# An order of TensorE's work made by a model of the engines, in place of fixed quarters of each key tile

## The reference, cut to what matters

```python
x = x + L0_xattn(layernorm(x), ctx)     # softmax(q k / sqrt(8)) v, then an output projection
x = x + L0_ffn(layernorm(x))            # 8 gated experts, hidden 192, capacity 512
x = x + L1_xattn(layernorm(x), ctx)     # softmax
x = x + L1_ffn(layernorm(x))            # 8 gated experts, hidden 256, two loops with rmsnorm
x = x + L2_xattn(layernorm(x), ctx)     # sigmoid(scores) v, no softmax
x = x + L2_ffn(layernorm(x))            # 8 experts with gelu, hidden 512
x = x + L3_xattn(layernorm(x), ctx)     # softmax
x = x + L3_ffn(layernorm(x))            # 8 gated experts with biases, hidden 256
```

## Time and profile before

| | |
|---|---|
| median of the runs shown | 4472.9 us (4469.91 to 4476.91, n = 3) |
| span of the profiled execution | 4471.6 us |
| ACT, PE, DVE, POOL busy | 87%, 86%, 65%, 18% of the span |
| mean granted TensorE clock | 0.968 of full |

### The profile page before, as it was taken

How to read it: one execution, slowest core, us unless ns; L and a number is a source line. 1 busy time by engine, 2 the same in 40 slices (tenths; PEclk the granted TensorE clock), 3 DMA queues, 4 the chain that set the end, 5 groups by cost and what they waited for, 6 DMA issues and landing times.

```text
span 4471.6 us, 69696 instructions
## 1 busy us (share of the span) xinstructions
PE 3844.3 (86%) x26742; PEld 881.7 (20%) x26742; DVE 2892.4 (65%) x5746; ACT 3897.2 (87%) x4328; POOL 820.2 (18%) x705
## 2 busy tenths in 40 slices
PE   8888888988889888898979998888888888888886
PEld 2121112211122211222212221111111111112112
DVE  6878898788877788877603332110785588877823
ACT  4689998899988899889899899989987889888994
POOL 3110001510035200252512111111001110044002
PEclk7699999999999999999999999999999999999998
DMA  6220001100021110111102221110011000010001
GB/s 157 56 63 25 12 12 33 35 12 12 17 60 31 46 25 17 33 36 34 33 19 63 64 71 27 39 40 17 14 31 27 27 12 12 14 43 24 5 1 50
DMA packets 124482, 151.31 MB, mean 34 GB/s; under 512 B 29272, under 2 KB 76384, under 8 KB 124080
## 3 DMA queue, kind: packets, MB, share of 16 engines
q1 hardware_dynamic: 123424, 146.41, 12.2%
q10 hardware_dynamic: 720, 0.40, 0.0%
HBM read 123.21 MB, written 23.51 MB: 33 GB/s over the span
## 4 chain that ended last, share of the span: by engine, by line
PE 49%; ACT 27%; DVE 13%; issue 6%; DMA 1%; SPq 0%; POOL 0%; ACTq 0%; POOLq 0%; DVEq 0%
PE av L884 20%; ACT prob L1045 17%; DVE mpart L1156 10%; PE scores L874 8%; PE side L906 5%; ACT above L1053 5%; PE scores L984 4%; PE side L1002 4%; PE side L984 2%; DVE above L1160 2%; PE scores L897 1%; ACT ag L1096 1%; ACT tx L1087 1%; PE side L874 1%; PE scores L1026 1%
## 5 line engine op out<-in xcount | busy, mean ns | idle before, releaser
L1045 ACT ACTIVATE prob<-scores 128x1024 f32<-128x1024 f32 x2998 | 2948.2, 1036 | 249.1 <-PE scores L874 221.8
L1156 DVE TENSOR_REDUCE mpart<-side 128x1 f32<-128x512 f32 (+1 forms) x3456 | 2132.8, 657 | 625.6 <-PE side L906 613.1
L884 PE MATMUL av<-prob,VA 128*9 128x512 f32 x6528 | 867.5, 604 | 40.5 <-ACT prob L1045 37.5
L884 PE MATMUL av<-prob,VB 128*9 128x512 f32 x6528 | 864.8, 602 | 18.7 <-ACT prob L1045 17.9
L874 PE MATMUL scores<-QP,KA 32*128 32x512 f16 x2996 | 562.0, 390 | 145.8 <-ACT above L1053 81.7
L874 PE MATMUL scores<-QP,KB 32*128 32x512 f16 x3000 | 554.3, 385 | 144.3 <-ACT above L1053 71.1
L906 PE MATMUL side<-KA,QP 32*128 32x512 f16 (+1 forms) x2112 | 618.1, 390 | 41.9 <-DVE mpart L1156 34.2
L906 PE MATMUL side<-KB,QP 32*128 32x512 f16 (+1 forms) x2112 | 578.1, 379 | 35.8 <-DVE mpart L1156 32.9
L1160 DVE CUSTOM_DVE_ANT_0 above<-side,above 128x512 f32<-128x512 f32 x768 | 516.3, 686 | 79.3 <-PE side L906 65.2
L1053 ACT ACTIVATE above<-scores 128x1024 f32<-128x1024 f32 x384 | 394.1, 1026 | 113.1 <-DVE mpart L1160 59.0
L1045 ACT ACTIVATE prob<-side 128x1024 f32<-128x1024 f32 x266 | 288.5, 1085 | 24.3 <-PE scores L874 23.8
(11 more groups left out here) (197 smaller groups left out, 2713.0 us busy)
## 6 DMA issues: line engine op xcount, KB each, us to landing
cwb<-weights SPq DMA_DIRECT2D x80, 256.0 KB, 3.9
KA<-kstacks SPq DMA_DIRECT2D x384, 48.0 KB
KB<-kstacks SPq DMA_DIRECT2D x384, 48.0 KB
Fin<-in_Fin SPq DMA_DIRECT2D x64, 256.0 KB, 2.8
kstacks<-hi SPq DMA_DIRECT2D x100, 128.0 KB, 2.4
ctxc<-in_ctxT SPq DMA_DIRECT2D x36, 256.0 KB, 3.0
hT<-in_mask SPq DMA_DIRECT2D x16, 400.2 KB, 3.5
kstacks<-lo SPq DMA_DIRECT2D x50, 128.0 KB, 2.6
```

Source lines behind the costliest of these rows:

```text
L884: last = pe.matmul(AV[ROWS * h:ROWS * h + VC, :], V[l % 2][:, kt, g * HG + h, :], prob[:, (e + h // 2) % RING, (h % 2) * QB:(h % 2) * QB + ...
L1045: act.activation(prob[:, e % RING, :], pair.rearrange("p a b -> p (a b)"), ACT.Exp if softmax(l) else ACT.Sigmoid, scale=SCALE).then_inc(s ...
L1156: dve.tensor_reduce(part, bank, AX.X, ALU.max).then_inc(sem["red"], 1)
```

## The change

`attention_steps` no longer lays out quarters. A class `Plan` steps through time at build: for each engine it holds queues of steps in program order (`heads`), `steps_before` says what each step needs, HOLD how long it keeps its engine and SEEN how much later another engine sees its end. ScalarE, VectorE, GpSimd and SyncE take the step that became ready first. TensorE's next step is chosen by `choose`: with a due `up`, `kv` or `qproj` product first (unless an `av` is ready and a score isn't), then a difference, then a score, then other due background products if they fit before ScalarE runs dry (plus 0.4), then a `max` if it costs no extra time or VectorE is about to starve, then `av` if it fits before ScalarE runs dry (plus 0.4), then background that isn't due yet. `start` models three modes of the array (rows for scores and maxima, columns for `av`, full for the rest) and the time between them. The order in which these events happen in the model is the order of all five programs.

Further: experts are due evenly between tile 12 and tile 130 to 200 of the unit's 204 (FFN_TO by unit), `kv` products between tile 24 and 280 (before: one per tile, six tiles apart for layer 3); `up`, `kv` and `qproj` planned this way always go to the ring of pairs, in the `by_dve` units too; `max` items go by key chunk first and by query block second; a phase's maxima have no window; `fina` waits for the last reduction by one semaphore; the load of `Wo` waits for `resid` where it waited for `oproj`. `opening_steps` and the end of unit 7 keep their lists. The steps themselves, their number and their shapes stay as they are.

```diff
-HALVES = [[(qt, c, 2 * half + j) for qt in range(QT) for c in range(2 * NDIF, NCH) for j in range(2)] for half in range(2)]
+HALVES = [[(qt, c, 2 * half + j) for c in range(2 * NDIF, NCH) for qt in range(QT) for j in range(2)] for half in range(2)]
...
-def in_pairs(what, key):
-
+def in_pairs(s):
+
+    if s.home:
+        return s.home == "pair"
+    what, key = s.what, s.key
     if what == "up":
         return not by_dve(*key[:2])
     return what in ("score", "dif") or what == "kv" and key[0] < 3 or what == "qproj" and key[0] in (-2, -1, 0, 1, 2, 5)
...
-COST = dict(red=0.62, both=0.7, resid=0.7, sum=0.7, sumsq=0.7, yadd=0.7, norm=0.35, rden=0.3, finc=0.7, fina=0.3, finb=0.2, routea=0.3, routeb=0.4,
-            routee=1.0, routef=0.5, routeg=0.5, routeh=0.5, routej=0.5, routek=0.5, routel=0.5, routec=1.0, routed=0.4, gatea=0.7, gateb=0.7,
-            ysum=0.7, upc=0.7)
-Q = 4 * KT
-
-PACE = {3: (1.3, True), 4: (1.5, True)}
-
-LEAD, END = 12, 3
-
...
-        kt, q = t // 4 % KT, t % 4
...
-        if q in (0, 2):
-            half = q // 2
-            for i in ((), (0, 1))[q == 0] if wide(t // Q, kt) else (half,):
-                out.append(Step("PE", "score", (t // Q, kt, i)))
-                out.append(Step("ACT", "exp", (t // Q, kt, i)))
-            due = has and ahead and ahead[0][0] <= t + 1 and not ready[0] and not ready[1]
-            if has:
-                find(1 - half, t, 5 if t >= window(p)[1] - END else 1 if half and due else 2)
-        if q == 3:
-            if kt:
-                out.append(Step("PE", "av", (t // Q, kt - 1)))
-            elif t // Q > first:
-                out.append(Step("PE", "av", (t // Q - 1, KT - 1)))
-            if has and ahead and ahead[0][0] <= t and not ready[0] and not ready[1]:
-                d = ahead.pop(0)[1]
-                out.append(Step("PE", "dif", (p, d)))
-                out.append(Step("ACT", "relu", (p, d)))
-                ready[DIFS[d][1]].append(t + 5)
-            if has:
-                find(0 if len(single[0] + both[0]) > len(single[1] + both[1]) else 1, t, 1)
...
+HOLD = dict(
+    PE=dict(av=0.853, up=0.858, down=0.858, kv=0.858, qproj=0.858, oproj=0.89, logit=0.79, oT=0.39, xT=0.39, oflip=0.39, yT=0.39, flipmax=0.39,
+            cwT=0.34, count=0.4),
+    ACT=dict(exp=0.905, relu=0.905, drain=0.48, qsplit=1.33, kc=0.59, rexp=0.14, msum=1.45, gelu=3.2),
+    DVE=dict(red=0.607, both=0.615, norm=0.21, rden=0.17, fina=0.26, finb=0.11, mean=0.1, routea=0.2, routeb=0.3, routee=0.56, routef=0.34, routeg=0.34,
+             routeh=0.33, routej=0.2, routek=0.17, routel=0.3, routec=0.9, routed=0.3, bqs=0.27, b1s=0.22, kc=0.67),
+    POOL=dict(gateb=2.83, hscale=2.3, ksplit=1.82, fill=0.56, zcopy=0.56, var=0.16, rstd=1.0, square=1.0, scale=1.0, center=1.0),
+    SP={})
+USUAL = dict(PE=0.858, ACT=0.494, DVE=0.607, POOL=1.22, SP=0.9)
+SEEN = dict(PE=0.32, ACT=0.165, DVE=0.12, POOL=0.1, SP=2.5)
+ROW, ROW_SEEN, ROW_DRAIN = 0.216, 0.445, 0.1
+FROM_ROW, FROM_AV, FROM_FULL = 0.0, 0.126, 0.2
+def steps_before(s):
...
+    if w == "exp":
+        t = KT * key[0] + key[1] - RING // 2
+        return [("score", key), ("av", (t // KT, t % KT))]
+    if w == "av":
+        return [("exp", key + (1,))] + [("drain", (key[0] - 1,))] * (key[1] == 0)
+    if w == "drain":
+        return [("av", key + (KT - 1,)), ("oT", (key[0] - 1,))]
+    if w == "relu":
+        return [("dif", key)] + [("red", (key[0], i)) for i in both_of(key[1] - 1)] * (key[1] > 0)
+    if w == "red":
+        return [("max", key)] + [("relu", (key[0], ITEM_DIF.get(key[1])))] * (key[1] >= FIRST_BOTH) + [("fina", (key[0] - 1,))]
...
+        self.paced = {}
+        for u in units:
+            if u:
+                work = [s for s in streams[FINISH] if s.eng == "PE" and s.key[0] == u - 1 and s.what in ("up", "down")]
+                self.paced.update({(s.what, s.key): NG * u * KT + FFN_FROM + (FFN_TO[u - 1] - FFN_FROM) * i / len(work) for i, s in enumerate(work)})
+        for l in range(4):
+            work = [s for s in streams[NEXT_KV] if s.eng == "PE" and s.key[0] == l]
+            self.paced.update({(s.what, s.key): 8 * (l - 1) * KT + KV_FROM + (KV_TO - KV_FROM) * i / len(work) for i, s in enumerate(work)})
...
+    def start(self, mode, group=None):
+
+        t = self.t
+        if mode == "row":
+            t = max(t, self.group[group])
+            return max(t, self.until + {"row": 0.0, "col": FROM_AV, "full": FROM_FULL}[self.mode])
+        if self.mode == "row":
+            return max(t, self.drained)
+        return max(t, self.until + (0.0 if self.mode == mode else FROM_AV if self.mode == "col" else FROM_FULL))
+
+    def row(self, s, groups, start):
+        for g in groups:
+            self.group[g] = start + ROW
+        self.drained = max(self.drained if self.mode == "row" else 0.0, start + ROW + ROW_DRAIN)
+        self.mode, self.t, self.until = "row", start, start
+        self.finished(s, start + ROW_SEEN)
+
+    def other(self, s, mode, start):
+        hold = HOLD["PE"].get(s.what, USUAL["PE"])
+        self.mode, self.t, self.until = mode, start, start + hold
+        self.finished(s, start + hold + (0.25 if mode == "col" else SEEN["PE"]))
+
...
+    def placed_at(self, s):
+
+        if s.what in ("up", "kv", "qproj"):
+            return s._replace(home="pair")
+        return s
+
+    def choose(self):
...
+        for i in (FINISH, NEXT_KV):
+            if self.lag(i) >= 0 and not (av and score is None):
+                s = self.placed_at(self.heads["PE"][i][0])
+                if s.home == "pair" and self.can(s):
+                    return self.issue_back(i, self.start("full"))
...
+        wake = None
+        reserved = 0
+        late = 1e9 if self.stalled() else self.dry("ACT")
+        for i in (MAXIMA, OUTPUT, FINISH, NEXT_KV):
+            lag = self.lag(i)
+            if lag >= 0:
+                s = self.placed_at(self.heads["PE"][i][0])
+                if s.home != "pair" and (s.what != "down" or s.key[-1] == 0):
+                    reserved = 1
+                if not av and self.can(s):
+                    start = self.start("full")
+                    hold = HOLD["PE"].get(s.what, USUAL["PE"])
+                    if i in (MAXIMA, OUTPUT) or start + hold + FROM_FULL + ROW_SEEN <= late + BACK_LATE + LAG * lag:
+                        return self.issue_back(i, start)
+        if self.p is not None and len(self.side) > reserved and self.side[0][1] <= self.t and not self.widening:
+            best = None
+            for half in range(2):
+                for q in (self.both[half], self.single[half]):
+                    if q:
+                        s = Step("PE", "max", (self.p, q[0]))
+                        if q is self.both[half] and self.done.get(("relu", (self.p, ITEM_DIF[q[0]])), 1e9) > self.t + 0.3:
+                            continue
+                        if self.can(s):
+                            start = self.start("row", ITEMS[q[0]][2])
+                            if best is None or start < best[0] - 1e-6:
+                                best = start, q, s
+            if best:
+                start, q, s = best
+                starving = self.dry("DVE") < self.t + DVE_LOW
+                if av:
+                    starving = self.dry("DVE") < self.start("col") + HOLD["PE"]["av"] + FROM_AV + ROW_SEEN - STARVE
+                free = self.mode == "row" and start + ROW + ROW_DRAIN <= self.drained + SLIP
+                if free or starving or self.mode == "row" and not av:
+                    if start <= self.t + EPS:
+                        q.popleft()
+                        self.take_bank(s)
+                        self.row(s, (ITEMS[s.key[1]][2],), start)
+                        self.heads["DVE"][ATTEND].append(Step("DVE", "red", s.key))
+                        self.issued += s.key[1] < FIRST_BOTH
+                        if not (self.single[0] or self.single[1] or self.both[0] or self.both[1] or self.dif < len(DIFS)):
+                            self.next_maxima()
+                        return None
+                    wake = start
+                    if self.mode == "row" and start < self.drained:
+                        return start
+        if av:
+            start = self.start("col")
+            if start + HOLD["PE"]["av"] + FROM_AV + ROW_SEEN <= late + AV_LATE:
+                if start <= self.t + EPS:
+                    self.avs.popleft()
+                    self.other(av, "col", start)
+                    return None
+                return start
...
+EPS = 0.002
+AHEAD = 0.0
+LAG, EARLY = 0.1, 0.0
+STARVE, SLIP = 0.3, 0.03
+FFN_FROM, FFN_TO, KV_FROM, KV_TO = 12, [130, 130, 180, 180, 130, 130, 200], 24, 280
+DVE_LOW, AV_LATE, BACK_LATE = 0.5, 0.4, 0.4
+def attention_steps(units):
+    return Plan(list(units)).steps()
...
-                    for i in (len(HALVES[0]) - 1, FIRST_BOTH - 1, FIRST_BOTH + len(BOTH[0]) - 1, len(ITEMS) - 1):
```

(10 more changed lines are left out.)

421 lines of the change are left out of this document (340 added, 81 removed).

## The result

The changed kernel takes 4408.4 us in the median (4405.4 to 4413.1) against 4472.0 for the kernel before on the same chip: a ratio of 0.9854, with a 95% interval from 0.984 to 0.9868. It is faster, by 64 us and not by the 252 that I forecast, and lies 8 us above the upper end of the range.

A forecast was written before the change was run, and what follows sets the result against it. The prediction took no engine as the bound alone; they wait for each other in turn. Its terms, 138 + 104 + 0 + 10 = 252 us off 4471.6, gave 4220, with a range from 4110 to 4400.

The forecast's parts named there:

- What bounds the kernel: Whole kernel: no engine is the bound alone, they wait for each other in turn; ScalarE's floor is 110.4 us a phase.
- The order in quiet tiles: 23 phases beside which maxima are found: reordered steps gain 6.0 us each, from 121.6 to 115.6, 138 in all.
- Background: Products beside softmax phases: spread where ScalarE has work left, they cost a quarter less of 417.8 us, a gain of 104.
- Pairs for `up`, `kv`, `qproj` with VectorE: Units emptied by VectorE: 0 in p16 to p19 (bounds -20 and +19), 10 us gained in p20 to p23 (0 to 30).
- Small edits: Item order, `fina` semaphore, `Wo` load: nothing counted separately; opening (163 us) and end after p31 (88 us) unchanged, 0.
- Rival E: Row, column and full work: shorter bursts pay change-over gaps more often, costing 163 of the 252 us: 4383; chance 0.05.
- Rival A: VectorE's banks decide: quiet phases gain 2 us (46), background half (52), p20 to p23 10: 4364; chance 0.14.
- Rival B: Close to the floors: ScalarE runs nearly without gaps, 372 us gained, 4100, quiet phases 112 or less; chance 0.12.
- C: `max` steps: scores behind late maxima wait and ScalarE runs dry; at 0.08 us longer each, 4544; chance 0.08.
- D: Whole kernel: no effect, events keep nearly the quarters' order or gains and extra drains cancel: 4472; chance 0.04.
- the clock: Units with gelu: no gain counted; at most 54 us could come back if evenly paced products held 2.4 GHz, to 4166.

The follow-up runs named there:

- a_chunks: The changed kernel with the items in the old order, query block first: 4411.2 us, 0.9859 of before.
- a_side_wide: The changed kernel with `up`, `kv`, `qproj` of VectorE-emptied units back in single banks and, in p15 to p22, a tile's two scores together: 4357.5 us, 0.9727.
- a_av: The changed kernel with `av` over 448 of 512 queries, the last 64 left out: 4338.5 us, 0.9689 of before.
- b_av: The kernel before with `av` over 448 of 512 queries, the last 64 left out: 4416.7 us, 0.9869 of before.

## Why the prediction was wrong, step by step

**What bounds the kernel:** right that no engine does alone (shares of 34% and 24% in the old order), wrong in what a looser order would turn to. I saw ScalarE at its floor next; TensorE, with the time between its kinds of work, was nearer (42% against 23% and 23% under the plan).

**The order in quiet tiles,** 23 x 6.0 = 138: right where it can be read alone. p7 and p27 gave 6.5 and 5.8 against 121.6 and 122.4. The six units with softmax gave 105 in all, with the same 85 in five of them whether they carry eight experts or four, so the gain is this term's and not the experts'. That it came to 105 and not to 138 stays open: tiles with products may have gained less, or `kv` and the other work of a unit's end may have become dearer, as p2 and p3 hint. It is not spread evenly either: unit 6 gave 38, units 1, 2 and 3 gave 8, 14 and 8.

**Background,** 104: this step failed. "If products go where ScalarE has work left ... the pass costs ScalarE's 40.3 and not TensorE's 53.3." ScalarE's spare work was the wrong cover. Half of the experts cost 149.3 us before and 149.5 after in the five units, and 57 and 69 in p16 to p23: the term was worth nothing where I had 104. TensorE's busy time falls with them by 147 and 153, ScalarE's by 109 and 104, so the price went by TensorE. I had named that bound, nothing, and set it against a floor that asked only whether ScalarE had room, not whether TensorE did. Why TensorE had none is argued from rows and not shown by a run of its own: its busy 101.1 of 121.6 leaves out the time between kinds of work. What I should have summed is its sequence in a tile with a product, an estimate: scores to `av` to scores 0.31 + 0.98, scores to product again 0.31, product to scores 1.03, some 2.6 us before any maximum, against ScalarE's 1.86 for two exponentials.

**Pairs for `up`, `kv`, `qproj` with VectorE,** 0 with bounds of -20 and +19: mis-sized. p16 to p19 lost 34 us. The price of the placement is 12 us in the old order, inside my bounds, but 38 under the plan, outside them; I priced it as if the tile's order stood still. And I missed that the plan would break the two scores which stood together: keeping them together gained 18 us more (51 bursts a phase had become 69 to 77 in p16 to p19). p20 to p23 gave nothing of the 10. The 0.3 us behind my upper bound has no row: a copy lasts 0.69 us, an exponential 1.02.

**Small edits:** a_chunks found nothing in the order of the items; the semaphore of `fina` and the load of `Wo` were not tried by themselves. The opening took 0.7 us more, and the end after p31 90.9 us where it took 88.6.

**Rivals.** Rival E had the time nearest to the result (4383), by luck for the most part: shorter bursts are what happened in p16 to p19, where they are worth some 18 us of its 163. Over all phases the plan's program has 2027 bursts and the quarters' 2085, so E's 1632 added breaks were not there, and from an `av` to the scores or maxima behind it the trace has 0.98 us in the median in both orders. The rule that I cited from the Trainium skill (TensorEngine Tiling (Array Packing), Key Properties), that a change of tiling mode drains the engine, agrees with a_side_wide's gain, though no run shows that a drain is the cause. Rival A (4364) foresaw a gain of the background's half, and its mechanism is not what happened: reductions give back 23% of what they are shortened by, and the phases quiet in both orders did not stay above 119. Rival B did not happen, since none came to 112, nor C, since ScalarE's wait for scores fell from 246 to 90 us. D is outside the interval. Of the clock no gain came: 0.968 before, 0.966 after. The units with gelu went from 0.95 and 0.95 to 0.97 and 0.96, unit 4 from 0.98 to 0.97 and unit 1 from 1.00 to 0.99.

In the sum: 138 + 104 + 0 + 10 - 0 = 252 forecast; 105 + 0 - 34 + 0 - 3 = 68 in the spans. Of the 184 us that are missing the background has 104, the placement 34 + 10, the order 33 and the two ends 3. With the background at nothing and the rest as forecast the kernel would have taken 4324, inside the range; what lay outside was that the placement went against me as well, which I had bounded at -20, and that the order brought less.

## What to carry to other kernels

Before a background product counts as hidden, sum the sequence of the engine that issues it, with the time between its kinds of work, and ask who is fed meanwhile: spare time on the consumer is no cover. A planner that orders one engine by priorities needs each priority weighed against the starving of every consumer; one rule without that test cost 49 us here, and one placement 38. Price a placement under the new order and not under the old one.

## What the runs showed of the hardware

TensorE's busy time is no measure of its work: the same 26742 records were busy for 3844, 4073 and 3987 us in three orders, and the one of 3987 is the fastest. The time from one kind of work to the next did not depend on the order: the medians of the two traces from an `av` to the scores or maxima behind it are 0.98 us, from scores or maxima to an `av` 0.31. And with `av` shortened by an eighth the granted clock of the profiled execution was 0.958 where it was 0.966, in the old order 0.957 where it was 0.968, so a little more of the time ran at 1.2 GHz and less at 2.4; with shorter exponentials it was 0.968 and 0.965. If the shorter `av` is what lowered it, which two orders suggest, a_av's and b_av's shares are too low rather than too high.
